# Reordering VectorE's loop body in a conv-attention and quantised-FFN block

## The chip, the cores and the metric

The kernel runs on one core of a Trainium2 chip. The metric is device time in microseconds, the median of several executions. A core has five engines with queues of their own: TensorE (PE) for matmuls, VectorE (DVE), ScalarE (ACT), GpSimd (POOL) and SyncE (SP), which issues DMAs. They meet only at semaphores.

## The reference

The input `x` is (16, 512, 24, 8) in f32: 16 images, 512 channels, 192 tokens each.

```python
# attention over channels, then over tokens, on xn = _ln_c(x)
avg, mx = jnp.mean(xn, axis=(2, 3)), jnp.max(xn, axis=(2, 3))
ca = sigmoid(mlp(avg) + mlp(mx))                  # mlp: relu(v @ fc1_w.T) @ fc2_w.T
v = xn * ca[:, :, None, None]
s = concat([mean(v, axis=1), max(v, axis=1)])     # 2 planes
x = x + v * sigmoid(conv7x7(s, sa_w))
# feed-forward on tokens, both weights ternary, both inputs rounded to 8 bits per token
t = _to_tokens(x)
t = t + bitlinear(gelu(bitlinear(_ln_t(t), w1)), w2)   # 512 -> 2048 -> 512
```

`bitlinear` finds the largest absolute value of a token's row, scales the row to 127, rounds it, and multiplies by the rounded weights.

## The kernel before, in words

Two images make a pair of 384 tokens, that is three tiles of 128 tokens (`Tile(pair, 0..2)`; `NT` is 3). There are eight pairs. A prologue prepares the weights and pairs 0 to 2 in part. Then `body` runs eight times on every engine, once per pair; I count them as bodies 0 to 7. Each engine's `body` is a list written out by hand, and that list is the order of its work. In the body of `pair`, four pairs are at work at once:

- `pair`: feed-forward of its last tile and the output products of all three;
- `nxt` (pair + 1): attention's result is added, the tokens are normalised and rounded, and the first product of tiles 0 and 1 is made;
- `att` (pair + 2): channel attention and the convolution;
- `fresh` (pair + 3): transposed from the input, and its channel statistics.

The last bodies leave out what has no pair: body 5 has no `fresh`, bodies 6 and 7 have no `att` either, body 7 no `nxt`.

VectorE's parts (L782 to L893). `token_max` (L787) takes channel maxima out of a PSUM bank. `hidden` (L794, L797) finishes fc1, behind which TensorE runs fc2, ScalarE a tanh. `split_gate` (L807, L809, L810) splits the channel gate in three bf16 parts by two subtractions whose operands lie in SBUF; TensorE's `turn_ca` waits for L810, and `spread_ca` spreads the gate over a PSUM bank. `scale_channels` (L816) multiplies by that bank. `channel_stats` (L774) and `aggregate` (L780) serve `fresh`. `split_stats` (L829, L830) has the form of `split_gate`; TensorE's `conv` waits for it (L1153). `sum_conv` (L835) gathers the convolution, ScalarE makes a tanh of it, and `token_gate` (L839) takes that. `add_attention` (L848) adds the attention to a tile `t`, with `bn_stats` (L850) and `bn_aggr` (L852). `centre` (L860 to L867) subtracts the mean, finds the largest value and makes the scale `q1`. `hidden_max` (L875) reads half of a tile's 2048 gelu results, `hidden_scale` (L883, L885) makes `q2` of the two halves. `add_ffn` (L892) adds the second product, in the PSUM bank `ps_o`, to `t`.

GpSimd's parts. `rstd2` (L447, L448) waits for `bn_aggr` and makes the reciprocal deviation that `centre` needs. `round_x` (L472) rounds what `centre` left. `round_g` (L483) waits for `q2` and rounds the gelu results in two instructions of 1024 columns, called halves here. `normalise1` (L453 to L460) normalises `fresh`.

TensorE's parts. `ffn_in` (L1177) is four blocks of four matmuls of 512 columns, `ffn_out` (L1188) sixteen matmuls, `fc1` L1117, `fc2` L1123, `turn_ca` L1130, `spread_ca` L1139, and several groups of transposes. In its body the order is ffn_in of tile 2, ffn_out of tile 0, ffn_in of `nxt`'s tile 0, ffn_out of tile 1 with fc1 before its last quarter, fc2, ffn_in of `nxt`'s tile 1 with `turn_ca` in its middle, the first two `spread_ca`, ffn_out of tile 2 with the third, and `conv` last.

Semaphores count the work done, and a wait names a count. A `link` on VectorE lets the next instruction start only when this one has ended; a `mark` only counts, and `chain.wait()` waits for all counted so far.

Of the kernel before, what the change touches and what calls it, by code (L numbers as in the profile page):

```python
# [5 lines left out]
def metaformer_kernel(nc, x, fc1_w, fc2_w, sa_w, w1, w2, out):  # L6
# [26 lines left out]
    NP = B // 2  # L33
# [11 lines left out]
    with ctx:  # L45
# [45 lines left out]
        xt = [sb(f"xt{i}", [P, NT, C]) for i in range(2)]  # L91
# [291 lines left out]
        def _(pool):  # L383
# [124 lines left out]
            def body(pair, attend, normalise, turn, split):  # L508
# [6 lines left out]
                if normalise:  # L515
                    round_x(Tile(nxt, 0))
                round_g(Tile(pair, 2))
                if normalise:
                    rstd2(Tile(nxt, 1))
                    round_x(Tile(nxt, 1))  # L520
                    round_g(Tile(nxt, 0))
                    rstd2(Tile(nxt, 2))
                    round_x(Tile(nxt, 2))
# [221 lines left out]
        def _(dve):  # L745
# [95 lines left out]
            def add_attention(tile):  # L841
# [6 lines left out]
                link(dve.scalar_tensor_tensor(t_tile, pv[par][:, s, :], sg[par][:, s:s + 1],  # L848
                                              xt[par][:, s, :], ALU.mult, ALU.add))
# [173 lines left out]
            def body(pair, attend, normalise, turn):  # L1023
                nxt, att, fresh = pair.plus(1), pair.plus(2), pair.plus(3)

                if pair.c > 0:
                    add_ffn(Tile(pair.plus(-1), 2))
# [9 lines left out]
                hidden_max(Tile(pair, 2), 1)  # L1037
                hidden_scale(Tile(pair, 2))
                if attend:
                    token_max(att, 2, V1_BANK[2])  # L1040

                add_ffn(Tile(pair, 0))
                if normalise:
                    add_attention(Tile(nxt, 1))
                    centre(Tile(nxt, 1))
                if attend:
                    token_max(att, 3, V1_BANK[3])
                if normalise:
                    hidden_max(Tile(nxt, 0), 0)
                    hidden_max(Tile(nxt, 0), 1)  # L1050
                if attend:
                    hidden(att)
                if normalise:
                    hidden_scale(Tile(nxt, 0))

                add_ffn(Tile(pair, 1))
                if normalise:
                    add_attention(Tile(nxt, 2))
                if attend:
                    split_gate(att)  # L1060
                if normalise:
                    centre(Tile(nxt, 2))
                    hidden_max(Tile(nxt, 1), 0)
# [3 lines left out]
                if turn:  # L1067
                    channel_stats(fresh, 0, 1)
                if attend:
                    scale_channels(Tile(att, 2), CA_BANK[2])  # L1070
                if turn:
                    aggregate(fresh, 0, 1)
# [3 lines left out]
                if attend:  # L1076
                    split_stats(att)
                if turn:
                    channel_stats(fresh, 2)
# [7 lines left out]
            add_ffn(Tile(Pair(NP - 1), 2))  # L1087
# [312 lines left out]
```

## Time and profile before

| what | value |
|---|---|
| median of 3 runs | 310.25 us (309.97 to 312.55) |
| the profiled execution | 312.61 us |
| its span, first to last instruction | 310.9 us |
| TensorE's mean granted clock | 0.941 of full speed |
| TensorE matmuls busy | 270.1 us, 87% |
| VectorE busy | 253.3 us, 81% |
| ScalarE, GpSimd busy | 217.2 us (70%), 162.8 us (52%) |

The span is the time that a profile's rows cover; the profiled execution is one more run, here a little longer than the median. Busy time says how much an engine had to do, not whether it set the end; for that the gaps between rows are read, and who ended each.

### The profile page before, as it was taken

To read this page: it belongs to the slowest core of one execution; us is meant where nothing else is said; L and a number is where in the kernel's file an instruction comes from. 1 tells how busy PE (TensorE), PEld (TensorE's weight loads), DVE (VectorE), ACT (ScalarE), POOL (GpSimd) and SP (SyncE) were. 2 spreads that over 40 slices of the span, in tenths; PEclk is the share of its full clock that TensorE was granted. 3 is DMA by queue.
4 is the path that set the end of the run, shared out by engine and by line. 5 is a ranking of instruction groups with operands and counts; after the bars stand their busy time and mean duration, and the time that the engine had idled before them with its cause. 6 is when DMAs were issued, how large, how long until landed. Compare 5 with 4: busy or idle time off the path is not lost.

```text
span 310.9 us, 5833 instructions
## 1 busy us (share of the span) xinstructions
PE 270.1 (87%) x1834; PEld 155.4 (50%) x1834; DVE 253.3 (81%) x558; ACT 217.2 (70%) x442; POOL 162.8 (52%) x261
## 2 busy tenths in 40 slices
PE   2665659686999999999999999999999987999974
PEld 2453544463546555645564556555555544444431
DVE  0756979989699989998999899899989997888410
ACT  2277488568586878687868777887678856676831
POOL 9503374515955395548564855576556663346410
PEclk9999775859699999999999999999999999799998
DMA  5899500001356048514941294339324723063593
GB/s 135 301 380 422 182 1 2 0 0 37 33 139 101 1 70 207 134 21 49 239 100 37 54 249 72 35 70 253 54 40 71 160 40 67 12 174 73 75 210 102
DMA packets 71078, 34.20 MB, mean 110 GB/s; under 512 B 52040, under 2 KB 68424, under 8 KB 70536
## 3 DMA queue, kind: packets, MB, share of 16 engines
q1 hardware_dynamic: 69384, 32.78, 44.4%
q10 hardware_dynamic: 1664, 1.05, 1.2%
q8 instruction: 15, 0.25, 0.3%
q14 instruction: 15, 0.12, 0.1%
HBM read 14.94 MB, written 6.29 MB: 68 GB/s over the span
## 4 chain that ended last, share of the span: by engine, by line
PE 39%; DVE 37%; issue 10%; ACT 7%; DMA 3%; POOL 2%; SPq 1%; ACTq 0%; DVEq 0%
PE ps_o L1188 12%; PE ps_h L1177 7%; DVE amax L875 7%; PE ps_t L1177 6%; DVE t L848 5%; PE small L1153 3%; PE front L1107 3%; DVE pv L816 3%; DVE st L850 3%; DVE amax L861 3%; DVE cen L860 2%; PE ps_t L1219 2%; DVE w_room L918 2%; PE front L1197 2%; DVE res L892 2%
## 5 line engine op out<-in xcount | busy, mean ns | idle before, releaser
L1188 PE MATMUL ps_o<-w2T,hq 128*128 128x512 f16 x384 | 92.6, 380 | 1.3 <-DMA hq<-w_raw 1.3
L483 POOL TENSOR_SCALAR w_room<-w_room,q 128x1024 f32<-128x1024 f32 x48 | 57.2, 1202 | 50.6 <-DVE q L885 50.1
L875 DVE TENSOR_REDUCE amax<-w_room 128x1 f32<-128x1024 f32 (+1 forms) x48 | 57.2, 1208 | 2.3 <-ACT w_room L542 2.2
L1177 PE MATMUL ps_h<-w1T,xq 128*128 128x512 f16 x208 | 55.9, 415 | 1.2 <-ACT xq L542 1.1
L1188 PEld LDWEIGHTS ps_o<-w2T,hq 128*128 128x128 f16 x384 | 36.3, 98 | 36.0 <-DMA hq<-w_raw 1.8
L542 ACT ACTIVATE w_raw<-w_room 128x1024 f16<-128x1024 f16 x48 | 50.4, 1052 | 0.6 <-POOL w_room L483 0.6
L542 ACT ACTIVATE w_room<-ps_h,s 128x512 f32<-128x512 f32 x52 | 35.0, 688 | 15.2 <-PE ps_h L1177 14.1
L1177 PE MATMUL ps_t<-w1T,xq 128*128 128x512 f16 x176 | 42.7, 386 | 0.0
L542 ACT ACTIVATE w_room<-ps_t,s 128x512 f32<-128x512 f32 x44 | 30.2, 687 | 8.2 <-PE ps_t L1177 5.6
L1177 PEld LDWEIGHTS ps_h<-w1T,xq 128*128 128x128 f16 x208 | 20.4, 105 | 24.7 <-issue 5.5
L542 ACT ACTIVATE junk_m<-front 128x192 bf16<-128x192 f32 x64 | 20.6, 332 | 16.0 <-DVE pooled L787 16.0
L892 DVE SCALAR_TENSOR_TENSOR res<-ps_o,s,t 128x512 f32<-128x512 f32 x24 | 18.0, 749 | 13.4 <-PE ps_o L1188 13.4
L1177 PEld LDWEIGHTS ps_t<-w1T,xq 128*128 128x128 f16 x176 | 17.3, 100 | 20.8 <-issue 2.5
L472 POOL TENSOR_SCALAR cen<-cen,q 128x512 f32<-128x512 f32 x24 | 16.6, 692 | 20.4 <-DVE q L867 20.4
L848 DVE SCALAR_TENSOR_TENSOR t<-pv,sg,xt 128x512 f32<-128x512 f32 x24 | 26.1, 1088 | 0.3
L1097 PE MATMUL front<-id,x_in 128*128 128x128 f32 x96 | 17.8, 326 | 7.0 <-DMA x_in<-in_x 6.1
L774 DVE BATCH_NORM_STATS2 st<-xt 128x6 f32<-128x512 f32 x24 | 15.8, 684 | 7.5 <-ACT xt L542 7.5
L1107 PE MATMUL front<-id,v 128*128 128x128 f32 x96 | 17.8, 308 | 3.9 <-ACT w1T L542 1.6
L542 ACT ACTIVATE w_room<-front 128x512 f32<-128x512 f32 x24 | 14.0, 585 | 8.9 <-PE front L1197 8.9
L787 DVE TENSOR_REDUCE pooled<-front 128x2 f32<-128x384 f32 x32 | 17.7, 553 | 2.7 <-PE front L1107 1.7
L460 POOL TENSOR_SCALAR v<-xt,minus_mean,rs 128x512 f32<-128x512 f32 x24 | 19.1, 797 | 1.4
L1097 PEld LDWEIGHTS front<-id,x_in 128*128 128x128 f32 x96 | 14.1, 172 | 10.7 <-issue 8.9
(126 smaller groups left out, 456.2 us busy)
## 6 DMA issues: line engine op xcount, KB each, us to landing
out<-w_room SPq DMA_DIRECT2D x16, 384.0 KB, 3.3
x_in<-in_x SPq DMA_DIRECT2D x14, 384.0 KB, 5.1
w_room<-in_L_ffn_w SPq DMA_DIRECT2D x4, 1024.0 KB, 8.9
w_raw<-in_L_ffn_w SPq DMA_DIRECT2D x4, 1024.0 KB, 12.1
x_in<-in_x ACTq DMA_DIRECT2D x2, 384.0 KB, 4.0
hq<-w_raw SPq DMA_TRANSPOSE x48, 3.1
fc_raw<-in_L_conv_fc_w ACTq DMA_DIRECT2D x2, 128.0 KB, 4.3
taps_rev<-in_L_conv_sa_w SPq DMA_DIRECT2D x2, 0.2 KB
```

What stands on the lines that cost most here:

```text
L460: pool.tensor_scalar(v1[:, s, :], xt[pair.par][:, s, :], minus_mean[:, s:s + 1], rs1[:, s:s + 1], ALU.add, ALU.mult).then_inc(normed, 1)
L472: pool.tensor_scalar(c[:, :], c[:, :], q1[tile.par][:, 0:1], MAGIC, ALU.mult, ALU.add).then_inc(cen_rounded, 1)
L483: pool.tensor_scalar(part, part, q2[tile.par][:, 0:1], MAGIC, ALU.mult, ALU.add).then_inc(g_rounded, 1)
L542: act.activation(out_ap, in_ap, func, **more).then_inc(signal, 1)
L787: dve.tensor_reduce(pooled[:, k, 0:2], front[bank][:, 0:TOK].rearrange("p (i t) -> p i t", i=2), AX.X, ALU.max).then_inc(max_ready, 1)
L848: link(dve.scalar_tensor_tensor(t_tile, pv[par][:, s, :], sg[par][:, s:s + 1], xt[par][:, s, :], ALU.mult, ALU.add))
L875: chain.mark(dve.tensor_reduce(amax2[:, i:i + 1], w1_room[:, first + i * F // 2:first + (i + 1) * F // 2 + i], AX.X, ALU.max, apply_absolu ...
L892: dve.scalar_tensor_tensor(res[tile.par][:, :], ps_o[:, :], s2[tile.third][:, 0:1], t[tile.pair.par][:, tile.s, :], ALU.mult, ALU.add).the ...
L1097: last = pe.transpose(front[bank][:, tile_cols(k)], x_in[tile.pair.par][:, k, tile_cols(tile.s)], id32[:, :])
L1107: last = pe.transpose(front[bank][:, tile_cols(s)], v1[:, s, tile_cols(k)], id32[:, :])
L1177: last = pe.matmul(banks[b], xq[tile.pair.par][:, tile.s, k, :], w1T[:, k, b * 512:(b + 1) * 512], start=(k == 0), stop=(k == NC - 1))
L1188: last = pe.matmul(ps_o[:, :], hq[tile.par][:, k, :], w2T[:, k, :], start=(k == 0), stop=(k == NF - 1))
```

## The change

Only the order of instructions changes, on VectorE and on GpSimd. On VectorE the attention add of `nxt`'s tile 1 moves ahead of `hidden_scale(pair, 2)`, with a `token_max` between it and its `bn_stats`; that of tile 2 moves ahead of `hidden_scale(nxt, 0)`, and with that ahead of `add_ffn(pair, 1)` and of `split_gate`. `hidden_max(nxt 0, 0)` moves ahead of the last `token_max`. The first two `scale_channels` move ahead of `hidden_max(nxt 1, 0)`, the third ahead of the first two `channel_stats`. `add_ffn(pair, 2)` moves from the start of the next body to behind `split_stats`. On GpSimd `rstd2` of tiles 1 and 2 moves ahead of the `round_g` that stood before it.

```diff
@@ gpsimd body @@
                 if normalise:
                     round_x(Tile(nxt, 0))
+                    rstd2(Tile(nxt, 1))
                 round_g(Tile(pair, 2))
                 if normalise:
-                    rstd2(Tile(nxt, 1))
                     round_x(Tile(nxt, 1))
+                    rstd2(Tile(nxt, 2))
                     round_g(Tile(nxt, 0))
-                    rstd2(Tile(nxt, 2))
                     round_x(Tile(nxt, 2))
@@ vector, add_attention @@
-            def add_attention(tile):
+            def add_attention(tile, between=None):
...
-                link(dve.scalar_tensor_tensor(t_tile, pv[par][:, s, :], sg[par][:, s:s + 1],
-                                              xt[par][:, s, :], ALU.mult, ALU.add))
+                chain.mark(dve.scalar_tensor_tensor(t_tile, pv[par][:, s, :], sg[par][:, s:s + 1],
+                                                    xt[par][:, s, :], ALU.mult, ALU.add))
+                if between:
+                    token_max(*between)
+                chain.wait()
                 link(dve.bn_stats(st2[:, :], t_tile))
@@ vector body @@
-                if pair.c > 0:
-                    add_ffn(Tile(pair.plus(-1), 2))
                 if normalise:
                     token_gate(nxt)
...
                 hidden_max(Tile(pair, 2), 1)
+                if normalise:
+                    add_attention(Tile(nxt, 1), (att, 2, V1_BANK[2]) if attend else None)
                 hidden_scale(Tile(pair, 2))
-                if attend:
-                    token_max(att, 2, V1_BANK[2])
 
                 add_ffn(Tile(pair, 0))
                 if normalise:
-                    add_attention(Tile(nxt, 1))
                     centre(Tile(nxt, 1))
+                    hidden_max(Tile(nxt, 0), 0)
                 if attend:
                     token_max(att, 3, V1_BANK[3])
                 if normalise:
-                    hidden_max(Tile(nxt, 0), 0)
                     hidden_max(Tile(nxt, 0), 1)
                 if attend:
                     hidden(att)
                 if normalise:
+                    add_attention(Tile(nxt, 2))
                     hidden_scale(Tile(nxt, 0))
 
                 add_ffn(Tile(pair, 1))
-                if normalise:
-                    add_attention(Tile(nxt, 2))
                 if attend:
                     split_gate(att)
                 if normalise:
                     centre(Tile(nxt, 2))
-                    hidden_max(Tile(nxt, 1), 0)
                 if attend:
                     scale_channels(Tile(att, 0), CA_BANK[0])
                     scale_channels(Tile(att, 1), CA_BANK[1])
+                if normalise:
+                    hidden_max(Tile(nxt, 1), 0)
+                if attend:
+                    scale_channels(Tile(att, 2), CA_BANK[2])
                 if turn:
                     channel_stats(fresh, 0, 1)
-                if attend:
-                    scale_channels(Tile(att, 2), CA_BANK[2])
-                if turn:
                     aggregate(fresh, 0, 1)
...
                 if attend:
                     split_stats(att)
+                add_ffn(Tile(pair, 2))
                 if turn:
                     channel_stats(fresh, 2)
```

The lines of the changed file stand up to three further down: L850 to L893 become L853 to L896.

VectorE in the middle of a body, from `hidden` to the last subtraction of `split_gate`. In these rows `lim` and `q_1` are `hidden_scale`, `res` is `add_ffn`, `t` the attention add, `ca_row` is `split_gate`. Before:

```order
L794 TENSOR_SCALAR hid_r<-small 64x4
L797 TENSOR_TENSOR hid<-hid_r 64x2
L883 TENSOR_SCALAR lim<-amax 128x1
L885 RECIPROCAL q_1<-lim 128x1
L892 SCALAR_TENSOR_TENSOR res<-ps_o,s_1,t 128x512
L848 SCALAR_TENSOR_TENSOR t<-pv,sg,xt 128x512
L850 BN_STATS st<-t 128x6
L852 BN_AGGR mv_1<-st 128x2
L807 TENSOR_SCALAR ca_row<-ca_tanh 128x8
L809 TENSOR_TENSOR ca_row<-ca_row 128x8
L810 TENSOR_TENSOR ca_row<-ca_row 128x8
```

After:

```order
L794 TENSOR_SCALAR hid_r<-small 64x4
L797 TENSOR_TENSOR hid<-hid_r 64x2
L848 SCALAR_TENSOR_TENSOR t<-pv,sg,xt 128x512
L853 BN_STATS st<-t 128x6
L855 BN_AGGR mv_1<-st 128x2
L886 TENSOR_SCALAR lim<-amax 128x1
L888 RECIPROCAL q_1<-lim 128x1
L895 SCALAR_TENSOR_TENSOR res<-ps_o,s_1,t 128x512
L807 TENSOR_SCALAR ca_row<-ca_tanh 128x8
L809 TENSOR_TENSOR ca_row<-ca_row 128x8
L810 TENSOR_TENSOR ca_row<-ca_row 128x8
```

The attention add with its statistics now stands ahead of `hidden_scale` and `add_ffn`; what stands directly before `split_gate` is `add_ffn` instead of the statistics.

VectorE at the end of a body, from the scale `q_1` of tile 2 to the second `hidden_max` of the next pair's tile 1 (`amax` from `w_room`); `pv` is `scale_channels`, `st` and `mv` the channel statistics. Before:

```order
L867 TENSOR_SCALAR q_1<-rec,rs_1 128x1
L875 TENSOR_REDUCE amax<-w_room 128x1
L816 ISA pv,ch_stat<-v,front 128x512
L816 ISA pv,ch_stat<-v,front 128x512
L774 BN_STATS st<-xt 128x6 x2
L816 ISA pv,ch_stat<-v,front 128x512
L780 BN_AGGR mv<-st 128x2 x2
L875 TENSOR_REDUCE amax<-w_room 128x1
```

After:

```order
L870 TENSOR_SCALAR q_1<-rec,rs_1 128x1
L816 ISA pv,ch_stat<-v,front 128x512
L816 ISA pv,ch_stat<-v,front 128x512
L878 TENSOR_REDUCE amax<-w_room 128x1
L816 ISA pv,ch_stat<-v,front 128x512
L774 BN_STATS st<-xt 128x6 x2
L780 BN_AGGR mv<-st 128x2 x2
L878 TENSOR_REDUCE amax<-w_room 128x1
```

The first `hidden_max` has moved from in front of all three `scale_channels` to behind the second, and the two `channel_stats` from in front of the third to behind it.

GpSimd in the same body: `w_room` is `round_g(pair, 2)` in two halves, `ve` and `rs_0` are `rstd2` of the next pair's tile 1, `cen` is `round_x`. Before:

```order
L483 TENSOR_SCALAR w_room<-w_room,q_0 128x1024 x2
L489 TENSOR_SCALAR s_2<-lim,w_unit 128x1
L447 TENSOR_SCALAR ve<-mv_0 128x1
L448 TENSOR_TENSOR rs_0<-ve,half_pow 128x1
L472 TENSOR_SCALAR cen<-cen,q_0 128x512
```

After:

```order
L447 TENSOR_SCALAR ve<-mv_0 128x1
L448 TENSOR_TENSOR rs_0<-ve,half_pow 128x1
L483 TENSOR_SCALAR w_room<-w_room,q_0 128x1024 x2
L489 TENSOR_SCALAR s_2<-lim,w_unit 128x1
L472 TENSOR_SCALAR cen<-cen,q_0 128x512
```

`rstd2` now comes before the rounding of the gelu results; for tile 2 and `round_g(nxt, 0)` it is the same.

## Rows read from the trace of the kernel before

**Rows 1.** The page: busy time and its share of the span by engine.

```profile
PE 270.1 (87%) x1834; PEld 155.4 (50%) x1834; DVE 253.3 (81%) x558; ACT 217.2 (70%) x442; POOL 162.8 (52%) x261
```

**Rows 2.** Timeline of TensorE, body 3 (start us, us, engine, line, operation, count, [idle before]).

```profile
171.46 1.89 PE L1177 MATMUL ps_h<-w1T,xq 128*128 128x512 f16 x8
...
187.16 0.61 PE L1117 MATMUL small<-pooled,fc1T 128*64 128x4 f32 x8
...
192.39 0.40 PE L1130 MATMUL small<-idb,ca_row 128*128 128x128 bf16 x4 [0.21 <-DVE ca_row L810]
...
194.35 0.59 PE L1139 MATMUL front<-caT,img_pick 128*128 128x512 bf16 x2
...
200.66 0.61 PE L1153 MATMUL small<-ch_stat,band 128*128 128x3 bf16 x18 [0.37 <-DVE ch_stat L830]
...
201.74 1.89 PE L1177 MATMUL ps_h<-w1T,xq 128*128 128x512 f16 x8
```

**Rows 3.** Timeline of VectorE, body 3, same columns.

```profile
181.34 1.56 DVE L848 SCALAR_TENSOR_TENSOR t<-pv,sg,xt 128x512 f32<-128x512 f32 x1
...
183.67 0.18 DVE L852 BATCH_NORM_AGGREGATE mv<-st 128x2 f32<-128x6 f32 x1
...
188.72 0.22 DVE L883 TENSOR_SCALAR lim<-amax 128x1 f32<-128x1 f32 x1
...
189.72 1.17 DVE L848 SCALAR_TENSOR_TENSOR t<-pv,sg,xt 128x512 f32<-128x512 f32 x1
...
191.65 0.18 DVE L852 BATCH_NORM_AGGREGATE mv<-st 128x2 f32<-128x6 f32 x1
191.75 0.16 DVE L807 TENSOR_SCALAR ca_row<-ca_tanh 128x8 f32<-128x8 f32 x1
...
194.06 1.21 DVE L875 TENSOR_REDUCE amax<-w_room 128x1 f32<-128x1024 f32 x1
...
201.92 0.17 DVE L835 TENSOR_REDUCE conv_sum<-small 128x3 f32<-128x9 f32 x1 [0.72 <-PE small L1153]
```

**Rows 4.** Timeline of GpSimd, body 3, same columns.

```profile
175.03 0.55 POOL L448 TENSOR_TENSOR rs<-ve,half_pow 128x1 f32<-128x1 f32 x1
175.68 1.11 POOL L483 TENSOR_SCALAR w_room<-w_room,q 128x1024 f32<-128x1024 f32 x1
...
183.94 0.48 POOL L447 TENSOR_SCALAR ve<-mv 128x1 f32<-128x1 f32 x1 [0.90 <-DVE mv L852]
...
189.23 2.64 POOL L483 TENSOR_SCALAR w_room<-w_room,q 128x1024 f32<-128x1024 f32 x2 [2.37 <-DVE q L885]
...
192.20 0.19 POOL L447 TENSOR_SCALAR ve<-mv 128x1 f32<-128x1 f32 x1
192.47 0.67 POOL L448 TENSOR_TENSOR rs<-ve,half_pow 128x1 f32<-128x1 f32 x1
```

**Rows 5.** Timeline of VectorE, the end of body 5.

```profile
260.15 1.01 DVE L829 TENSOR_TENSOR ch_stat<-ch_stat 128x6 f32<-128x6 f32 x1 [0.22 <-ACT junk_p L542]
261.19 1.06 DVE L830 TENSOR_TENSOR ch_stat<-ch_stat 128x6 f32<-128x6 f32 x1
```

**Rows 6.** Timeline of GpSimd, the end of body 5.

```profile
260.03 2.21 POOL L483 TENSOR_SCALAR w_room<-w_room,q 128x1024 f32<-128x1024 f32 x2 [4.24 <-DVE q L885]
```

**Rows 7.** Timeline of TensorE, bodies 0 and 5.

```profile
96.93 0.63 PE L1117 MATMUL small<-pooled,fc1T 128*64 128x4 f32 x8
...
103.76 0.60 PE L1139 MATMUL front<-caT,img_pick 128*128 128x512 bf16 x2
...
109.81 0.62 PE L1153 MATMUL small<-ch_stat,band 128*128 128x3 bf16 x18 [0.37 <-DVE ch_stat L830]
...
262.31 0.61 PE L1153 MATMUL small<-ch_stat,band 128*128 128x3 bf16 x18 [1.41 <-DVE ch_stat L830]
...
263.40 2.79 PE L1177 MATMUL ps_h<-w1T,xq 128*128 128x512 f16 x8
```

**Rows 8.** Windows on TensorE's granted clock (PEclk), body 5.

```profile
264.00:265.00 1.00, 1.00 (x4) 0.61 0.11 20
```

More of the change, by code:

```diff
@@ L1066, in body @@
                     scale_channels(Tile(att, 1), CA_BANK[1])
-                if turn:
-                    channel_stats(fresh, 0, 1)
+                if normalise:
+                    hidden_max(Tile(nxt, 1), 0)
                 if attend:
@@ L1071, in body @@
                 if turn:
+                    channel_stats(fresh, 0, 1)
                     aggregate(fresh, 0, 1)
@@ L1086, in _ @@
                 body(Pair(c), c < NP - 2, c < NP - 1, c < NP - 3)
-            add_ffn(Tile(Pair(NP - 1), 2))
         @block.tensor
```

## The prediction

> **What bounds the kernel now.** First read the busy shares [rows 1]: TensorE 87%, VectorE 81%. Neither alone is the limit, so the waits of one loop body decide. Bodies 1 to 4 are alike; I take body 3, from the first matmul of its ffn_in to that of the next body, 171.46 to 201.74, 30.28 us [rows 2]. TensorE works through its list from 171.46 with no gap the profile shows until 192.39, where turn_ca has waited for split_gate's last subtraction (L810). The second gap stands ahead of the convolution at 200.66, behind split_stats. From the spread_ca pair at 194.35 on it has work of its own; the convolution's wait is what ends last.
>
> Next the VectorE timeline [rows 3]. The stretch that feeds the convolution begins with the hidden_max at 194.06 and goes on without a hole: 200.66 - 194.06 = 6.60 us for one hidden_max, three scale_channels, two bn_stats, the second hidden_max, the scale and split_stats. I call this the tail. In body 3 the first scale_channels finds its PSUM bank filled, because that hidden_max ran first. The only hole is 0.72 before sum_conv at 201.92.
>
> Then GpSimd beside VectorE [rows 3, 4]. The attention add (L848) is one shape, yet takes 1.56 at 181.34 and 1.17 at 189.72. Rounding of g started at 189.23, its two halves cost 2.64 instead of the 2.21 of body 5's pair [rows 6], and the 0.43 lost there is what the add ran ahead of the second half. Body 5 shows it more sharply [rows 5, 6]: the two subtractions of split_stats, six columns wide, take 1.01 and 1.06; they end 1.13 and 2.22 behind the start of the rounding at 260.03, as its two halves end. The eight-column subtraction L810 has the same form: two operands of SBUF.
>
> The Trainium skill's "SBUF — State Buffer", Who interferes with whom, says that a VectorE instruction with two SBUF inputs and a GpSimd instruction that reads SBUF exclude each other, whoever starts first holding the port for its whole instruction. The rows of body 5 agree (1.01 and 1.06). Were it shared in proportion instead, six columns would cost next to nothing and the first rival below would be the forecast.
>
> **The change part by part.** No instruction is added or removed; all prices are shifts.
>
> Attention add of tile 1: ahead of hidden_scale(pair,2), so ahead of that tile's rounding. The nearest undisturbed duration is the 0.75 left of 1.56 and 1.17 when the lengthening is taken off (1.17 less the 0.43 of the rounding); gain 0.81. Bounds: 0 to 0.81. The token_max put between it and its bn_stats only fills the add's own drain. GpSimd's rstd2 moves ahead of the rounding, otherwise centre would wait for it.
>
> Attention add of tile 2: ahead of hidden_scale(nxt,0), gain 0.43 by the same rows; bounds 0 to 0.43.
>
> add_ffn(pair,2) in the convolution's hole: the add and the third bn_stats together fit in the time that conv needs, so sum_conv is not later; token_gate comes forward until it meets ScalarE's tanh, 0.2 to 0.4 sooner. GpSimd is busy with normalise1 and rstd2 of tile 0 then, and VectorE waits for that result; I book 0. Bounds -0.4 to +0.1.
>
> Are these gains on the path? No: VectorE's next stop is hidden(att), which needs fc1, and TensorE has fc1 at 187.16 because its list is full from 171.46 on [rows 2]. VectorE used to arrive at about 188.45 (0.27 before L883 at 188.72) [rows 3]; less the 0.81 it is there at 187.64 or earlier, and fc1's result comes at 187.82 (next part), so it idles 0.2 or more. Here everything that was gained ends.
>
> **From fc1 to the convolution, new order.** fc1 starts 187.16, lasts 0.61, is seen 0.05 later: 187.82. hidden's two small operations take about 0.27, an estimate from the 0.16 of L807, another of their size [rows 3]. From an attention add's start to its aggregate it is 191.65 - 189.72 = 1.93, less the 0.43 of the rounding 1.50. So the aggregate starts at A = 187.82 + 0.27 + 1.50 = 189.59. Now hidden_scale and add_ffn(pair,1) stand between it and split_gate. The next instruction starts 0.10 behind an aggregate (191.65 to 191.75), and from the scale's L883 to what follows add_ffn it is 1.00 (188.72 to 189.72) [rows 3]. So split_gate starts at A+1.10, and its first subtraction at A+1.29, by 0.19 for the step before it.
>
> GpSimd: rstd2 starts 0.27 behind the aggregate (183.67 to 183.94), its power 0.27 later (192.20 to 192.47), and a rounding whose input is there 0.65 behind that (175.03 to 175.68) [rows 3, 4]: A+1.19. In the old order rounding was past its first half before the bn_stats, and split_gate met no rounding at all. Now the rounding is 0.10 ahead of the subtraction; in body 5 it was 0.12 ahead and held [rows 5, 6]. So both subtractions are held by one half each: L810 ends at A + 1.19 + 2.22 = A + 3.41 = 193.00, and turn_ca starts 0.06 behind that, as conv at 262.31 behind 261.19 + 1.06 [rows 5, 7]: 193.06. It started at 192.39: 0.67 later, although its input used to sit behind an attention add that took 1.17. This wait is new in kind; behind it on TensorE are ffn_in's blocks 2 and 3, spread_ca, ffn_out and conv.
>
> From turn_ca to spread_ca 1.96 (192.39 to 194.35) [rows 2]: 195.02. Its first matmul fills the bank in about 0.38 (half of the pair's 0.59 and the drain; an estimate), seen 0.04 later: 195.44. scale_channels now comes first in the tail, the hidden_max behind the second one, so nothing of the tail runs before this. centre and q1 of tile 2 end at about 194.7 behind the held subtraction, so they do not decide. Tail 6.60: conv at 202.04 instead of 200.66, 1.38 later, say 1.4, and the next ffn_in as much. Bounds for the body: at best, no hold, spread_ca starts sooner by turn_ca's idle time, 0.21 as shown and up to 0.16 more, since a matmul's end is modelled (1.89 stands for eight that follow each other 1.73 apart); the tail starts at 194.40 and the price is still 0.34; at worst centre is held too (third rival), 2.3.
>
> Body 0 [rows 7]: fc1 at 96.93, by the same steps turn_ca at 102.83 (5.90 behind fc1), spread_ca 104.79 instead of 103.76, tail from 105.21, conv 111.81 instead of 109.81: 2.0. Its hidden_max used to fill the wait for spread_ca, so here even the case without a hold loses 103.76 + 0.42 + 6.60 - 109.81 = 0.97. Body 5 has a shorter tail with its own waits; I take half of a middle body, 0.7, from bounds of -0.8 and 1.4. Bodies 6 and 7 have no convolution and TensorE's own list decides; 0. Prologue 0.
>
> Sum: 2.0 + 4 x 1.4 + 0.7 = 8.3 us. Against the profiled execution, 312.61 with a span of 310.9, that is 320.9; against the median of the three runs, which is 2.36 lower, 310.25 + 8.3 = 318.6.
>
> **The rivals.**
>
> Split_gate gets through (chance 0.19). The margin is 0.10 us. If the first subtraction comes before the rounding has the port, at most the second is held for a half, until about A+2.35 = 191.94, and TensorE reaches turn_ca at about 192.02 anyway. Then only the filler's loss is left: 0.97 + 4 x 0.34 - 0.8 = 1.5, so 311.8; with centre of tile 2 held instead, up to 315. For: 0.10 is thin. Against: body 5, 0.12.
>
> Faster (0.08). VectorE's work itself, not the stop at fc1, sets the body; then the 0.81, the 0.43 and some 0.3 of the hole come off, about 1.5 per body, also all that TensorE's gaps hold. Five bodies: 7.5, 302.8. It decides if the tail can start before 194.06, which needs the spread_ca pair earlier than a full TensorE list gives. For: no VectorE row from 181.34 to the tail's end is preceded by idle time [rows 3]. Against: TensorE has none up to turn_ca either [rows 2], and the tail now waits for it.
>
> The clock falls (0.23). My forecast leaves TensorE idle from about 200.3 to 202.1 and then in conv's tiny matmuls to 203.3. In body 5 it stood idle 1.41 before conv at 262.31 [rows 7], and then the granted clock was 0.61 and lower, the 1.2 GHz level, from 264 on [rows 8]; the eight matmuls at 263.40 took 2.79 instead of 1.89 [rows 2, 7], and the next eight about as much more, 1.7 together. In bodies 0 to 4 the idle before conv was 0.37 and the clock stayed at 2.4 GHz. One such fall per body would add up to 5 x 1.7 = 8.5: 327.1; one or two, 320 to 322.
>
> The Trainium skill's "TensorE: Matmul & The Clock Gate", Part 1, says that idleness brings the gate back to half rate. By it this rival adds to the 8.3; the rows of body 5 agree with the rule.
>
> Centre of tile 1 is held as well (0.08). It starts at A+1.10 of its own aggregate against the rounding's A+1.19; by the same reckoning it is first, by 0.09. If it is not, it loses a half, 1.1, the token_max behind it comes too late for ScalarE's means, and fc1 slips by about 0.9 per body: 8.3 + 6 x 0.9 = 13.7, 324.0.
>
> **How the numbers follow.** The forecast has 0.42, the rivals 0.19, 0.08, 0.23 and 0.08. Predicted is the forecast's 318.6. Range: down to the first rival, 311.5, and up to falls of the clock in every body, 327.0; this leaves out the faster case and little else. About 1%, 3.1 us, is what a measurement of this kernel can tell from no change. Within 1%: most of the first rival, 0.18. Faster 0.08, the rest, 0.74, slower.
>
> **What would show it.** Right: L809 and L810 at about 1.0 each in bodies 0 to 5 (0.19 and 0.17 now), the rounding beside them; the idle time of TensorE before turn_ca near 1.0 and before conv near 1.8; an idle VectorE before hidden_r and before the first scale_channels; the attention adds at 0.75; bodies 31.7 long. Wrong: L809 at 0.19 points to the first rival; a body under 30 us to the faster one; matmuls of ffn_in at double length right behind conv to the clock; centre (L863 there) at 1.5 to the last. If the scale_channels does not wait for spread_ca, the step that carries everything has failed.

## The result, and the profile after

The changed kernel takes 323.64 us in the median of 4 runs (322.65 to 324.43), the kernel before 310.62 beside it. The ratio is 1.0395, with a 95% interval of 1.0354 to 1.0436: 4% slower. The span of the profiled execution is 322.7, against 310.9. The sums below explain these two spans; the rest of the 13.0 by which the medians differ lies in the scatter from run to run.

First the page of the changed kernel: the busy line that answers to [rows 1], and the clock in 40 slices.

```profile
PE 271.3 (84%) x1826; PEld 156.4 (48%) x1834; DVE 256.7 (80%) x558; ACT 218.1 (68%) x442; POOL 157.2 (49%) x261
...
PEclk9855756778999989997999799999997999999998
```

TensorE has the same work within 1.2 us, VectorE is busy for 3.4 more, GpSimd for 5.6 less, with the same instructions; the span is 11.8 longer. So work was not added, waits were. Each digit of PEclk is the mean granted clock of a fortieth of the span, in tenths of full speed; the 8 behind the first 9999 and the three 7s after it mark the four slow stretches that the next rows show.

TensorE's timeline, the body that answers to body 3 of [rows 2] and the conv behind the next one. Columns as there.

```profile
178.72 0.61 PE L1152 MATMUL small<-ch_stat,band 128*128 128x3 bf16 x18 [1.63 <-DVE ch_stat L830]
...
179.81 2.92 PE L1176 MATMUL ps_h<-w1T,xq 128*128 128x512 f16 x8
182.52 2.59 PE L1176 MATMUL ps_t<-w1T,xq 128*128 128x512 f16 x8
184.95 0.60 PE L1196 MATMUL front<-id,res 128*128 128x128 f32 x4
...
197.17 0.63 PE L1116 MATMUL small<-pooled,fc1T 128*64 128x4 f32 x8
...
203.12 0.40 PE L1129 MATMUL small<-idb,ca_row 128*128 128x128 bf16 x4 [0.91 <-DVE ca_row L810]
...
212.24 0.61 PE L1152 MATMUL small<-ch_stat,band 128*128 128x3 bf16 x18 [1.63 <-DVE ch_stat L830]
...
213.32 1.89 PE L1176 MATMUL ps_h<-w1T,xq 128*128 128x512 f16 x8
...
244.07 0.61 PE L1152 MATMUL small<-ch_stat,band 128*128 128x3 bf16 x18 [1.63 <-DVE ch_stat L830]
```

Read the brackets first. Before turn_ca TensorE now stands idle 0.91 (0.21 before), and before conv 1.63 (0.37). From one conv to the next it is 212.24 - 178.72 = 33.52 here, and 244.07 - 212.24 = 31.83 in the next body; it was 30.28. The difference between these two bodies is in their first rows: at 179.81 eight matmuls are given 2.92 and the next eight 2.59, and turn_res follows at 184.95, 5.14 behind. At 213.32 the eight are 1.89 as before.

VectorE in the same body, what answers to [rows 3].

```profile
197.83 0.15 DVE L794 TENSOR_SCALAR hid_r<-small 64x4 f32<-64x4 f32 x1 [0.71 <-PE small L1116]
...
198.13 0.75 DVE L848 SCALAR_TENSOR_TENSOR t<-pv,sg,xt 128x512 f32<-128x512 f32 x1
...
199.65 0.18 DVE L855 BATCH_NORM_AGGREGATE mv<-st 128x2 f32<-128x6 f32 x1
...
200.72 0.17 DVE L807 TENSOR_SCALAR ca_row<-ca_tanh 128x8 f32<-128x8 f32 x1
200.92 1.05 DVE L809 TENSOR_TENSOR ca_row<-ca_row 128x8 f32<-128x8 f32 x1
202.01 1.06 DVE L810 TENSOR_TENSOR ca_row<-ca_row 128x8 f32<-128x8 f32 x1
...
205.50 0.69 DVE L816 CUSTOM_DVE_ANT_0 pv<-v,front 128x512 f32<-128x512 f32 x1 [0.61 <-remote]
```

GpSimd beside it, what answers to [rows 4].

```profile
199.92 0.19 POOL L447 TENSOR_SCALAR ve<-mv 128x1 f32<-128x1 f32 x1 [3.71 <-DVE mv L855]
200.19 0.55 POOL L448 TENSOR_TENSOR rs<-ve,half_pow 128x1 f32<-128x1 f32 x1
200.84 2.21 POOL L483 TENSOR_SCALAR w_room<-w_room,q 128x1024 f32<-128x1024 f32 x2
```

Both attention adds now take 0.75 (the one of tile 2 is the row at 198.13). VectorE idles 0.71 for fc1 before that. Then the rounding starts at 200.84, the first subtraction of split_gate (L809) at 200.92, and the two take 1.05 and 1.06 instead of 0.19 and 0.17. The first scale_channels, at 205.50, has waited 0.61.

The windows on TensorE's granted clock, one microsecond each, in the body with the slow matmuls and in the next, answer to [rows 8].

```profile
181.00:182.00 1.00, 1.00 (x4) 0.50 0.00 0
214.00:215.00 1.00, 1.00 (x6) 1.00 0.24 46
```

0.50 is the 1.2 GHz level, 1.00 the 2.4. Behind the convolutions at 111.79, 145.21, 178.72 and 244.07 the matmuls are slow, behind those at 212.24 and 275.85 they are not. I call such a slow stretch a fall of the clock.

### The profile page after: what moved, and what is told of

The parts are those of the page before. It is cut to its first block, busy times and chain, and to the rows that moved or that the text cites. A ratio compares the mean times of both kernels' runs of the same rounds, so it can differ in the third digit from the quotient of the medians.

```text
span 322.7 us, 5825 instructions
## 1 busy us (share of the span) xinstructions
PE 271.3 (84%) x1826; PEld 156.4 (48%) x1834; DVE 256.7 (80%) x558; ACT 218.1 (68%) x442; POOL 157.2 (49%) x261
## 3 DMA queue, kind: packets, MB, share of 16 engines
q10 hardware_dynamic: 1664, 1.05, 1.2%
## 4 chain that ended last, share of the span: by engine, by line
PE 47%; DVE 28%; issue 10%; ACT 4%; POOL 3%; DMA 3%; another core or an unknown queue 2%; SPq 1%; ACTq 0%; DVEq 0%; POOLq 0%
PE ps_o L1187 16%; PE ps_h L1176 10%; PE ps_t L1176 8%; DVE amax L878 3%; PE front L1106 3%; DVE pv L816 3%; DVE st L774 3%; DVE t L848 2%; PE small L1152 2%; PE front L1196 2%; DVE ca_row L809 2%; DVE st L853 2%; DVE w_room L921 2%; DVE amax L864 2%
## 5 line engine op out<-in xcount | busy, mean ns | idle before, releaser
L483 POOL TENSOR_SCALAR w_room<-w_room,q 128x1024 f32<-128x1024 f32 x48 | 55.5, 1166 | 20.9 <-DVE q L888 19.0
L1176 PE MATMUL ps_h<-w1T,xq 128*128 128x512 f16 x208 | 59.1, 433 | 1.3 <-ACT xq L542 0.7
L447 POOL TENSOR_SCALAR ve<-mv 128x1 f32<-128x1 f32 x24 | 5.2, 215 | 60.6 <-DVE mv L855 60.0
L1096 PE MATMUL front<-id,x_in 128*128 128x128 f32 x96 | 17.0, 313 | 6.2 <-DMA x_in<-in_x 5.7
L848 DVE SCALAR_TENSOR_TENSOR t<-pv,sg,xt 128x512 f32<-128x512 f32 x24 | 20.0, 835 | 0.3
L816 DVE CUSTOM_DVE_ANT_0 pv<-v,front 128x512 f32<-128x512 f32 x24 | 15.9, 683 | 5.2 <-remote 5.2
```

The source lines that it names most:

```text
L483: pool.tensor_scalar(part, part, q2[tile.par][:, 0:1], MAGIC, ALU.mult, ALU.add).then_inc(g_rounded, 1)
L816: dve.tensor_tensor_reduce(out=pv[tile.pair.par][:, tile.s, :], in0=v1[:, tile.s, :], in1=front[bank][:, :], scale=1.0, scalar=-3.0e38, op ...
L848: chain.mark(dve.scalar_tensor_tensor(t_tile, pv[par][:, s, :], sg[par][:, s:s + 1], xt[par][:, s, :], ALU.mult, ALU.add))
L1096: last = pe.transpose(front[bank][:, tile_cols(k)], x_in[tile.pair.par][:, k, tile_cols(tile.s)], id32[:, :])
L1176: last = pe.matmul(banks[b], xq[tile.pair.par][:, tile.s, k, :], w1T[:, k, b * 512:(b + 1) * 512], start=(k == 0), stop=(k == NC - 1))
```

## The experiments

The table has, for each kernel, the median beside the runs of before on the same chip, the length of a middle body as the distance between two conv starts, where no slow matmuls stand in it, the idle time before conv, and how many of the five convs that end bodies 0 to 4 have slow matmuls behind them in the one profile.

| kernel | median, before beside it | ratio [95%] | body | idle | slow |
|---|---|---|---|---|---|
| before | 310.62 | 1 | 30.28 | 0.37 | 0 |
| the change | 323.64, 310.62 | 1.040 [1.035, 1.044] | 31.83 | 1.63 | 4 |
| rounding waits for split_gate | 311.62, 311.75 | 1.002 [0.999, 1.005] | 30.74 | 1.63 | 0 |
| matmuls before conv | 319.40, 311.75 | 1.026 [1.021, 1.031] | 31.83 | none | 0 |
| tail as before | 317.26, 311.75 | 1.019 [1.013, 1.026] | 31.00 | 0.37 | 0 |
| tile 2's add as before | 312.64, 311.75 | 1.003 [1.000, 1.006] | 30.74 | 1.63 | 1 |
| rounding waits, tail as before | 307.77, 312.59 | 0.986 [0.982, 0.989] | 29.48 | 0.37 | 0 |
| tile 2's add and tail as before | 308.65, 312.59 | 0.988 [0.985, 0.991] | 29.63 | 0.37 | 0 |
| before, with the new tail alone | 315.76, 312.59 | 1.011 [1.008, 1.014] | 31.13 | 1.63 | 2 |
| matmuls before turn_ca | 324.42, 312.59 | 1.038 [1.034, 1.041] | 31.83 | 1.63 | 4 |
| before, with tile 1's add alone | 308.15, 312.26 | 0.988 [0.982, 0.993] | 29.63 | 0.37 | 0 |
| before, with add_ffn moved alone | 312.22, 312.26 | 0.999 [0.996, 1.001] | 30.29 | 0.37 | 0 |

### The hold taken away on GpSimd

```diff
                     rstd2(Tile(nxt, 2))
+                    if attend:
+                        wait(pool, ca_ready, pair.plus(2).at(1, 1))
                     round_g(Tile(nxt, 0))
```

VectorE's order stays as in the change; only the rounding starts later.

> The changed kernel with one wait more on GpSimd: the rounding of the next pair's tile 0 begins only when split_gate's last subtraction is done. VectorE's order is untouched. Theory (the two subtractions are held by the rounding, and that moves turn_ca, the spread and the convolution): L809 and L810 fall from 1.05 and 1.06 us to about 0.2 each, the idle time of TensorE before turn_ca (0.91) goes, a body without a fall of the clock is 30.6 to 30.8 instead of 31.83, and the time is about 316 (323.6 less 6 x 1.2), nearer 311 if the falls of the clock go too. Rival (the hold is a symptom and the body is set by the order of the tail alone): subtractions short, but the bodies stay at 31.8 and the time at 323.

The VectorE rows, timeline of this kernel: split_gate's subtractions (L811 and L812 in this file) and the first scale_channels.

```profile
193.46 0.17 DVE L811 TENSOR_TENSOR ca_row<-ca_row 128x8 f32<-128x8 f32 x1
193.67 0.17 DVE L812 TENSOR_TENSOR ca_row<-ca_row 128x8 f32<-128x8 f32 x1
...
196.96 0.69 DVE L818 CUSTOM_DVE_ANT_0 pv<-v,front 128x512 f32<-128x512 f32 x1 [1.30 <-PE front L1140]
```

TensorE's conv and the ffn_in behind it.

```profile
203.69 0.61 PE L1154 MATMUL small<-ch_stat,band 128*128 128x3 bf16 x18 [1.63 <-DVE ch_stat L832]
...
204.78 1.89 PE L1178 MATMUL ps_h<-w1T,xq 128*128 128x512 f16 x8
```

The subtractions are back at 0.17, the body is 30.74, 1.09 shorter than the change's. So the hold costs 1.09 per body, by a test that moves nothing on VectorE. The rest of the loss per body, 30.74 - 30.28 = 0.46, is still there, and so is the idle time before conv. The clock did not fall in the loop of this profile. I had expected 316 with the falls and nearer 311 without them; the time is 311.62.

### Tile 2's attention add as it was

```diff
                 if normalise:
-                    add_attention(Tile(nxt, 2))
                     hidden_scale(Tile(nxt, 0))
 
                 add_ffn(Tile(pair, 1))
+                if normalise:
+                    add_attention(Tile(nxt, 2))
...
                     round_x(Tile(nxt, 1))
-                    rstd2(Tile(nxt, 2))
                     round_g(Tile(nxt, 0))
+                    rstd2(Tile(nxt, 2))
```

> The changed kernel with tile 2's attention add back behind hidden_scale and add_ffn (and rstd2 of tile 2 back behind the rounding). Theory (its move ahead of hidden_scale is what put split_gate into the rounding): the attention add is held by 0.43 again, the subtractions are short, turn_ca is not waited for, a body without a fall of the clock is about 30.6, the time 316 or, without falls, 311; the same as with the rounding held back on GpSimd, by another way. Rival (the move of tile 2's add itself gains, and the loss is in other parts): no better than 323.

VectorE's timeline: the attention add of tile 2, and the two subtractions.

```profile
192.98 0.79 DVE L848 SCALAR_TENSOR_TENSOR t<-pv,sg,xt 128x512 f32<-128x512 f32 x1
...
194.83 0.19 DVE L809 TENSOR_TENSOR ca_row<-ca_row 128x8 f32<-128x8 f32 x1
195.06 0.17 DVE L810 TENSOR_TENSOR ca_row<-ca_row 128x8 f32<-128x8 f32 x1
```

The same body, 30.74, by the other way. The add's move caused the hold. It wasn't even held by the 0.43 that I expected: it took 0.79 and ran between the two halves of the rounding, which took 2.64 instead of 2.21.

### The tail's order as it was

```diff
                     centre(Tile(nxt, 2))
+                    hidden_max(Tile(nxt, 1), 0)
                 if attend:
                     scale_channels(Tile(att, 0), CA_BANK[0])
                     scale_channels(Tile(att, 1), CA_BANK[1])
-                if normalise:
-                    hidden_max(Tile(nxt, 1), 0)
-                if attend:
-                    scale_channels(Tile(att, 2), CA_BANK[2])
                 if turn:
                     channel_stats(fresh, 0, 1)
+                if attend:
+                    scale_channels(Tile(att, 2), CA_BANK[2])
+                if turn:
                     aggregate(fresh, 0, 1)
```

> The changed kernel with the first hidden_max of tile 1 back ahead of the three scale_channels, and the channel statistics as before: only the tail's order is undone. Theory (VectorE idles 0.6 before the first scale_channels, which waits for the spread, and the moved hidden_max used to fill that): the hidden_max starts where the idle time began, the convolution starts 6.60 behind it, 0.8 sooner per body, so 31.0 without a fall, and the time is about 319. Rival (the scales first release TensorE's transposes sooner, and that is worth more than the filler): bodies 31.8 or longer, 323 or more.

VectorE's timeline in one body: the second subtraction, the hidden_max, the first scale_channels.

```profile
194.54 1.06 DVE L810 TENSOR_TENSOR ca_row<-ca_row 128x8 f32<-128x8 f32 x1
...
197.34 1.21 DVE L878 TENSOR_REDUCE amax<-w_room 128x1 f32<-128x1024 f32 x1
198.47 0.68 DVE L816 CUSTOM_DVE_ANT_0 pv<-v,front 128x512 f32<-128x512 f32 x1
```

The subtraction is still held (1.06), but the hidden_max begins as soon as q1 is done, and no idle time stands before the scales. The body is 31.00, 0.83 shorter, the number expected. And with 0.37 of idle time before conv no middle body has slow matmuls. The expected 319 had left the falls in; the time is 317.26. It isn't lower still because body 5 is longer with this order, and a fall behind its conv is back; more on that below.

### The new tail alone, on the kernel before

This puts the same lines, with the signs turned, into the kernel before.

> The kernel before with the tail's new order alone: the first hidden_max of tile 1 behind the second scale_channels, the channel statistics behind the third. Theory (filler lost): the tail of 6.60 starts 0.42 behind spread_ca's start, at 194.77 instead of 194.06 in body 3's numbers, so bodies of 31.0, body 0 longer by 1.0, time 314.5 to 316; the idle time before conv goes from 0.37 to about 1.1. Rival (the order of the tail costs nothing by itself, the loss comes only with the held subtractions): bodies 30.3, time 311 to 312.

```profile
198.32 0.21 DVE L867 TENSOR_SCALAR q<-rec,rs 128x1 f32<-128x1 f32 x1
199.16 0.69 DVE L816 CUSTOM_DVE_ANT_0 pv<-v,front 128x512 f32<-128x512 f32 x1 [0.62 <-PE front L1139]
```

These VectorE rows are q1 and the first scale_channels, 0.62 idle between them. The part costs 0.85 per body by itself (31.13 against 30.28). That is the 0.71 expected and 0.14 more, because from the first scale_channels to conv it is 205.90 - 199.16 = 6.74, where the old tail had 6.60. And it is this part alone that makes TensorE wait 1.63 before conv (I had expected 1.1); two convs in the profile have slow matmuls behind them. The rival falls.

### TensorE kept busy before conv

```diff
                 ffn_out(Tile(pair, 2), (3,))
                 if attend:
+                    wait(pe, g_ready, Tile(nxt, 2).at(FB, -3))
+                    for k in range(8):
+                        pe.matmul(ps_h[0][:, :], w1T[:, 0, 0:P], w1T[:, k % 4, 0:512], start=True, stop=True)
                     conv(att)
```

> The changed kernel with eight matmuls of 512 columns more per body on TensorE, ahead of conv, on constants, into a bank that the next ffn_in overwrites; their result is used nowhere. They fill the 1.63 us in which TensorE waits for split_stats. Theory (the idle time ahead of conv lets the granted clock fall, and each fall costs 1.7): no ffn_in behind a conv is slow (1.73 us for eight matmuls each time), the time falls by four falls of 1.7 less at most 0.2 per body for the matmuls: 317 to 318. Rival (ffn_in is slow for another reason, or the fall is set by the work before): the slow ffn_in stay, the time is 323 to 325.

TensorE's timeline: the eight new matmuls, conv behind them, ffn_in; then the eight and conv at the end of body 5.

```profile
205.46 1.89 PE L1374 MATMUL ps_h<-w1T 128*128 128x512 f16 x8
207.26 0.61 PE L1152 MATMUL small<-ch_stat,band 128*128 128x3 bf16 x18
...
208.34 1.89 PE L1176 MATMUL ps_h<-w1T,xq 128*128 128x512 f16 x8
...
269.13 1.89 PE L1374 MATMUL ps_h<-w1T 128*128 128x512 f16 x8
270.85 0.60 PE L1152 MATMUL small<-ch_stat,band 128*128 128x3 bf16 x18
```

The new matmuls fill the gap, conv has no idle time before it, and the middle body stays 31.83: there they cost nothing. In body 5 they do. The change has no idle time before that conv, so the eight matmuls only push it back, and body 5 is 31.76 long where that of the change is 30.08 without the clock's part; that is why the time is 319.40 and not the 317 to 318 that I expected. No matmuls behind a conv are slow, in any body of the loop. The kernel is 2.6% above its runs of before where the change is 4.0% above its own, and the medians, 319.40 against 323.64, differ by 4.2 us (5.4 when each is taken against the runs of before beside it). Its four runs lie within 0.17 us (319.37 to 319.54), where those of the change lie within 1.8. That fits a scatter that comes from the clock.

### TensorE kept busy before turn_ca

```diff
                 if attend:
+                    wait(pe, g_ready, Tile(nxt, 1).at(FB, -1))
+                    for k in range(4):
+                        pe.matmul(ps_t[0][:, :].bitcast(f32), w1T[:, 0, 0:P], w1T[:, k % 4, 0:512], start=True, stop=True)
                     turn_ca(att)
```

> The changed kernel with four matmuls of 512 columns more per body ahead of turn_ca (constants, result unused), which fill the 0.91 us that TensorE waits there; the 1.63 before conv stays. The version with the rounding held back had the same 1.63 before conv and no 0.91, and its clock did not fall in the loop. Theory A (both gaps in one body are needed for a fall): the falls go or become rare, the time is 317 to 320, bodies 31.8 to 32.0. Theory B (the gap before conv alone does it, and the other run had luck): three or four falls stay, 323.

TensorE's timeline: a slow ffn_in, the four new matmuls, the conv.

```profile
179.96 2.52 PE L1176 MATMUL ps_h<-w1T,xq 128*128 128x512 f16 x8
...
202.20 1.03 PE L1357 MATMUL ps_t<-w1T 128*128 128x512 f16 x4
...
212.39 0.61 PE L1152 MATMUL small<-ch_stat,band 128*128 128x3 bf16 x18 [1.63 <-DVE ch_stat L830]
```

The gap before turn_ca is filled, and four convs still have slow matmuls behind them (2.52 in the row at 179.96). Theory A falls: with the gap before turn_ca filled the falls stay, with the one before conv filled they go.

### Does the clock always fall behind such a gap?

The kernel with the rounding held back was profiled a second time, in an execution that took 313.88.

> The changed kernel with GpSimd's rounding held back, profiled once more. Its first profile had 1.63 us of idle time before each conv and no fall of the clock in the loop, where the changed kernel with the same 1.63 had four. If whether the clock falls behind such a gap varies from run to run, one to four slow ffn_in show up here; if it is fixed by this kernel's body of 30.74, none does again.

TensorE's timeline of this second profile.

```profile
113.32 3.48 PE L1178 MATMUL ps_h<-w1T,xq 128*128 128x512 f16 x8
```

Here the matmuls behind the conv that ends body 0 are slow, 3.48 for eight instead of 1.89; in the first profile none were. So the same program with the same 1.63 us has such falls in one execution and not in another. The conv that ends body 5 says the same: with 1.41 idle before it the matmuls behind it are slow in the kernel before, in the one with the tail as before and in the two below that move one part alone, and not slow in the two fastest versions. In the loops of these profiles no fall came without a gap, then, but a gap is not enough for one. What picks the body is open.

### The two remaining parts alone, on the kernel before

> The kernel before with one part of the change alone: tile 1's attention add ahead of hidden_scale, with the token_max in it, and rstd2 of tile 1 ahead of the rounding. Theory (VectorE's chain up to fc1 gets 0.8 us shorter and then waits for fc1, so what comes through is the 0.6 by which VectorE used to be late for fc1's result): bodies 29.6 to 29.7, VectorE idle before hidden, the time 308 to 309, nearly all that the best version gained. Rival (the gain of that version came from add_ffn of tile 2 in the convolution's hole): bodies 30.2, 312.

VectorE's timeline of the kernel with tile 1's add alone: the wait for fc1.

```profile
186.24 0.15 DVE L794 TENSOR_SCALAR hid_r<-small 64x4 f32<-64x4 f32 x1 [0.56 <-PE small L1119]
...
187.88 0.79 DVE L848 SCALAR_TENSOR_TENSOR t<-pv,sg,xt 128x512 f32<-128x512 f32 x1
...
189.72 0.20 DVE L809 TENSOR_TENSOR ca_row<-ca_row 128x8 f32<-128x8 f32 x1
189.95 0.17 DVE L810 TENSOR_TENSOR ca_row<-ca_row 128x8 f32<-128x8 f32 x1
```

VectorE idles 0.56 for fc1, split_gate meets no rounding, and the body is 29.63. This part is worth 0.65 per body, as expected, and all of it lies ahead of fc1: hidden starts 17.42 behind the last conv instead of 18.09, and from hidden to the next conv it is 12.21 instead of 12.20.

> The kernel before with one other part alone: add_ffn of tile 2 ahead of the convolution's sum. Theory: token_gate comes 0.3 sooner, GpSimd's v and rstd2 then hold centre and lim, so at most 0.3 per body is left: bodies 30.0 to 30.3, time 310.5 to 312.5. Rival: it alone gives the gain, 308 to 309.

VectorE and GpSimd of the kernel with add_ffn moved alone.

```profile
172.12 0.17 DVE L839 TENSOR_SCALAR sg<-sg_tanh 128x3 f32<-128x3 f32 x1 [0.24 <-ACT sg_tanh L542]
172.32 0.75 DVE L848 SCALAR_TENSOR_TENSOR t<-pv,sg,xt 128x512 f32<-128x512 f32 x1
...
174.05 0.74 DVE L860 TENSOR_SCALAR cen<-t,mv 128x512 f32<-128x512 f32 x1
```

```profile
172.23 0.19 POOL L453 TENSOR_SCALAR ve<-mv 128x1 f32<-128x1 f32 x1
172.50 0.97 POOL L454 TENSOR_TENSOR rs<-ve,half_pow 128x1 f32<-128x1 f32 x1
```

token_gate waits 0.24 for the tanh, the add comes 0.36 sooner than the 172.68 of the old order, but GpSimd's power takes 0.97 instead of 0.54 beside it, and then centre 0.74 instead of 0.48. The body is 30.29: nothing comes through.

### Versions that beat both kernels

Both losses taken out, in two ways: the rounding waits for split_gate and the tail is as before, or tile 2's add and the tail are both as before.

> Both losses taken out: GpSimd's rounding waits for split_gate, and the hidden_max of tile 1 is back ahead of the scales. Theory: VectorE has the 1.30 us before the first scale_channels free in the version with the wait alone, the hidden_max of 1.13 fits in, the convolution starts 1.1 sooner: bodies 29.6 (30.28 before), idle time before conv 0.5 to 0.7, time about 304 to 305, faster than before by some 2%. Rival (TensorE's or GpSimd's chain takes over as soon as VectorE is out of the way): bodies 30.2 or more, 309 to 311.

> The changed kernel with two of its parts undone: tile 2's attention add behind add_ffn again, hidden_max of tile 1 ahead of the scales again. What is left of the change is tile 1's attention add, hidden_max of tile 0 ahead of the last token_max, and add_ffn of tile 2 ahead of the convolution's sum. Theory: nothing holds split_gate, the hidden_max fills the wait of 0.89 for the spread, conv starts 1.1 sooner than with tile 2's add undone alone: bodies 29.6, time 304 to 305. Rival: as above, 309 to 311.

VectorE's timeline of the first: the hidden_max and the first scale_channels.

```profile
191.23 1.21 DVE L880 TENSOR_REDUCE amax<-w_room 128x1 f32<-128x1024 f32 x1
192.61 0.69 DVE L818 CUSTOM_DVE_ANT_0 pv<-v,front 128x512 f32<-128x512 f32 x1 [0.17 <-PE front L1140]
```

TensorE's conv.

```profile
198.09 0.61 PE L1154 MATMUL small<-ch_stat,band 128*128 128x3 bf16 x18 [0.37 <-DVE ch_stat L832]
```

The hidden_max fills the wait for spread_ca up to the last 0.17. The bodies are 29.48 and 29.63, and both versions are faster than the kernel before, by 1.4% (1.1 to 1.8) and 1.2% (0.9 to 1.5): clear of no change, but less than 2%. The bodies came out at the 29.6 that I expected, the times did not: I had put down 304 to 305, they are 307.77 and 308.65. A body gains 30.28 - 29.48 = 0.8 against the kernel before in the first version and 0.65 in the second, so five bodies give 4.0 and 3.3, and the medians differ by 4.8 and 3.9; the 6 to 8 us in my expectation never followed from its own bodies. The idle time before conv is 0.37, not the expected 0.5 to 0.7. The second version is no better than tile 1's add alone, which has the same body of 29.63, and the interval of the first overlaps with that of this single part as well.

## Why the prediction was right, and where it was not

**The stop at fc1.** Right in the place, wrong in one word. VectorE idles 0.71 before hidden; the prediction had 0.2 or more. That tile 1's add is free of the rounding is in its row (0.74 at 189.57). But the answer "No" to whether these gains are on the path is too strong. VectorE used to come to hidden at 188.46, 0.64 behind fc1's result at 187.82. So much of the 0.81 comes through, as the version with tile 1's add alone shows with 0.65; only the rest ends at fc1. The sum had it all the same, because it counts from fc1's result at 187.82.

**The hold of split_gate.** Right, to a tenth. From fc1's start to turn_ca's it is 203.12 - 197.17 = 5.95; the prediction had 5.90. Aggregate to rounding is 1.19 (199.65 to 200.84), as laid out; to L809 it is 1.27, two hundredths sooner than forecast, and the rounding still had the port with 0.08 in hand. Two experiments that remove the hold by different means shorten the body by 1.09 each. The margin was as thin as the prediction feared: at the end of body 5 a subtraction starts 0.06 behind a rounding of the same form and is not held (rows under the sum). The first rival's condition did not arise; its body of 30.62 was a good account of the version without a hold, 30.74.

**The filler of the tail.** Right. The first scale_channels waits 0.61 for the spread; from turn_ca to it 2.38, as forecast. Undoing this part alone gives back 0.83, adding it alone costs 0.85. Conv then follows 6.74 behind instead of 6.60, so the middle body grew by 1.55, not 1.4. What was not foreseen is that in body 5 the same order of the tail gains, see the sum.

**The sum.** Body 0: conv at 111.79, forecast 111.81; that they agree to 0.02 is partly luck, since fc1 came 0.18 sooner (96.75) and the way from there to conv was 0.16 longer. Bodies 1 to 4: 6.4 together without the clock (1.8 in body 1, 1.5 to 1.55 in the others), forecast 5.6. Body 5 is the term of the sum that was mis-sized: 0.7 was taken, but it ended 275.85 - 244.07 = 31.78 behind the conv before, 1.7 of it the clock's, against 31.32 before, so it is 1.2 shorter. The rows of the changed kernel show why.

```profile
275.42 0.17 DVE L829 TENSOR_TENSOR ch_stat<-ch_stat 128x6 f32<-128x6 f32 x1
275.62 0.17 DVE L830 TENSOR_TENSOR ch_stat<-ch_stat 128x6 f32<-128x6 f32 x1
```

These are split_stats' subtractions on VectorE at the end of body 5; GpSimd's rounding beside them starts behind the first:

```profile
275.56 2.23 POOL L483 TENSOR_SCALAR w_room<-w_room,q 128x1024 f32<-128x1024 f32 x2 [4.29 <-DVE q L888]
```

They take 0.17 each instead of the 1.01 and 1.06 of [rows 5], which I had used only as a yardstick and not as a cost that the new order takes away. In the old order split_stats waited 0.22 for ScalarE's last sum, and meanwhile the rounding started; now that sum is done before the rounding's scale is. The tail's order does this: with the tail as before, body 5 is 32.03 long and its two subtractions take 1.00 and 1.06 again. So the order that costs 0.83 in a middle body gains 1.95 in body 5. Without the clock the sum is then 2.0 + 6.4 - 1.2 = 7.2, against 8.3.

**The clock.** This is the step that failed. The prediction's text had TensorE idle from about 200.3 to 202.1 before conv and had the rows in which the clock fell behind 1.41 of such idle time, and yet left it at nothing in the 8.3, without a reason, and kept it as a rival of 0.23 on top. It came together with the forecast: four falls in the profiled execution (behind the convs that end bodies 0, 1, 2 and 4). Three cost 5.14 less the usual 3.45 = 1.7 each, the one behind body 0 took 4.79 and cost 1.3. The kernel before has one of 1.7, behind the conv that ends body 5, and the change has none there. Net that is 6.4 - 1.7 = 4.7. With it 7.2 + 4.7 = 11.9 us, and the spans differ by 11.8. The matmuls before conv show the cause, not only the coincidence. The median was right in sign and inside the range, 5.0 above the point. It was inside it because the upper bound allowed for falls that the forecast left out; and since the sum without the clock came 1.1 lower than forecast, part of the clock's 4.7 does not show in the miss.

**Centre of tile 1.** Not held, as forecast: it starts at 192.51, 0.11 ahead of the rounding (192.62), and takes 0.48; the rounding takes 2.45 instead of 2.21.

**Faster.** Its condition, a tail that starts before 194.06, did not arise in the change. What speaks for it in part is that tile 1's add alone gains 0.65 per body: VectorE did set the old body, up to the point where fc1 takes over.

**add_ffn in the hole.** Booked at 0, measured at 30.29 against 30.28.

## What to carry to other kernels

VectorE and GpSimd meet not only at semaphores, as these rows show, but also where both read operands in SBUF. So ask of each moved instruction not only what it escapes but what the instruction behind it now meets: two eight-column subtractions cost 1.05 us each here because a 1024-column rounding had started 0.08 before. An instruction that looks like a delay ahead of a wait may be the filler of that wait, so look whether the next one's input is there before pulling it forward. Undo the parts of a change in every stage of the loop before calling one a loss: the tail's order lost in the middle bodies and gained in body 5. And a gap of TensorE that is about to grow should be priced twice, once as the wait and once with the half clock behind it, if any gap of that length in the trace has that behind it.

## What the runs showed of the hardware

With 1.63 us idle before conv and then conv's small matmuls, the granted clock fell to the 1.2 GHz level behind four, four, two and one of five convs in profiles of different kernels, and behind none and one of five in two profiles of one and the same kernel. With 1.41 idle, before the conv that ends body 5, it fell in four profiles and not in two. With 0.37 idle, in six kernels, it fell behind none of five. Eight matmuls whose result nobody reads, put in the gap, removed the falls and cost no time where the gap was 1.63; in body 5, where there was none, they cost 1.7.

GpSimd's hold on the shared operands can be seen to begin later than its row starts, and not equally late for all operations. The rounding (L483) held a subtraction that started 0.08 behind it (L809 at 200.92, 1.05), and did not hold one that started 0.06 behind it (L830 at 275.62, 0.17). The normalising instruction (L460) started at 211.39; L829, 0.13 behind it, took 0.17, and L830, 0.33 behind it, took 0.46, until L460's first half was done. It goes the other way too: in body 3 of the version with add_ffn moved alone the power (L454), 0.54 otherwise, took 0.97 beside the attention add; VectorE was first there and GpSimd paid.
